# Attention with a pruned score mask: transposes and value products one unit later, the output copy in the slot of the last value products

## The chip, the core and the metric

One core of a Trainium2 chip runs the kernel. The metric is the device time of one execution in microseconds (us). The engines used are TensorE (PE in the profile; its weight loads are PEld), VectorE (DVE), ScalarE (ACT), GpSimd (POOL) and SyncE (SP), which issues all DMAs. Each engine works through its own program in order and is tied to the others by semaphores only.

## The reference, cut to what matters

```
x = in (8 batches, 512 tokens, 128 channels), f32;  xn = layernorm(x)
q, k, v = split(xn @ w_attn.T + b_attn);  16 heads of 8 channels
att = q @ k.T / sqrt(8), causal
S = relu(att of head 0), column 0 and diagonal set to 0
FF = cumulative sum of S down the rows, shifted by one row
att = att - FF                                    # the same FF for all heads
keep the 101 smallest FF of each row and the diagonal; the rest of att = -inf
y = softmax(att) @ v;  attn = y @ w_proj.T + b_proj
ffn = sum over the 2 chosen of 8 experts of gate * (relu(xn @ wi.T + bi + lora_e(xn)) @ wo.T + bo)
out = x + attn + ffn
```

## The kernel before, in words

The kernel takes the 8 batches one after the other. A batch's attention is cut into 44 **units** (`UNITS`, L58): a pair of a tile `a` of 128 queries (0 to 3) and so many heads that the scores fill one bank of PSUM: 4 heads for `a` = 0 (4 units), 2 for `a` = 1 (8 units), 1 for `a` = 2 and 1 for `a` = 3 (16 units each). `LAST` (L60) is the number of the last unit of each `a`: 3, 11, 27, 43. Four heads make a **group**; the group's last unit is marked in `ENDS_GROUP`.

Every engine's program is one loop over **slots** t (L514, L625, L902, L1144), one slot for each unit and some before and after. Unit u passes through these steps:

- PE, slot u, `score` (L851): the scores of unit u into one of three banks `ps_s`. It waits until VectorE has masked unit u-3 (L862).
- DVE, slot u (L1212): adds the mask, writes `ar` (a ring of 7) and the row maximum `mx`. POOL, slot u (L523), subtracts: the maximum minus the score.
- PE, slot u + LAG_T, `turn` (L868): transposes the unit into one of two banks `ps_t`; it waits for POOL (L871) and for the exponentials of unit u-2 (L875).
- ACT, slot u + LAG_T (L682): the exponentials, `pr` (a ring of 6).
- PE, slot u + LAG_P, `weigh` (L881): for the last unit of a group, the value products of four heads into the one bank `ps_o`. The first group of the next `a` waits until that bank was copied out (L887).
- ACT, slot LAST[a] + LAG_P + OUT_LAG (L694): copies `ps_o` to `out_t`, after the wait for all value products of that `a` (L696).
- PE, "ot{a}", slot LAST[a] + LAG_P + OT_LAG (L825): transposes `out_t`; DVE divides by the sums in the same slot (L1190). "yt{a}" (L831) comes two slots after it, "proj1" two more after yt3 (L84 to L86). "proj0" stands at slot 40.

In a slot PE does, in this order, score(t), turn(t - LAG_T), the jobs of the slot (`fill`), weigh(t - LAG_P). ACT does the jobs that it reads, the exponentials, the copy of `ps_o` if it is due, and then its part of the preparation of other batches (`act_prepares`). DVE does its jobs, the mask of unit t, and then preparation.

The jobs are everything that is no attention unit: the feed-forward part of the batch (z at slot 5, mask0 and mask1 at 7 and 8, the hidden layers h00 to h31 at slots 14 to 24, two products each from L807 and L811, down0 and down1 at 28 and 30), and the preparation of the next batches (s0 to s3 at 15 to 18, v at 16, f0 to f3 at 20 to 23, then on DVE and ACT a search for a threshold from slot 24 on, L1030 to L1061, and the choice of the largest values at slots 32 to 41; xt, q, k at 32, 34, 36; gate at 43, and its expert choice on DVE at slots 43 to 48). The search reads `nf`, which needs f3 on PE, DVE and POOL.

All jobs share two banks `ps_m`. `Plan` (L131 to L169) sorts the jobs by slot, within one slot by their place in the list (the feed-forward and output jobs stand ahead of the preparation), and gives the banks in turn; the two halves of a hidden layer keep one bank. A job waits until its bank's job before it has been read (L708).

SP issues the DMAs of the q and k stacks, x and the output (L417 to L425); the output's wait for proj0 and proj1.

Of the kernel before, what the change touches and what calls it, by code (L numbers as in the profile page):

```python
# [64 lines left out]
NS_RING, NT_RING, NM_RING = 3, 2, 2  # L65
NBANKS = NM_RING + NT_RING + NS_RING + 1
NA_RING, NP_RING = 7, 6
LAG_T, LAG_P = 3, 4
OUT_LAG, OT_LAG, YT_LAG = 1, 2, 4
TAIL = 13  # L70

QUAD = 4
# [1215 lines left out]
```

How the kernel before makes its waits and increments, by code:

```python
            def wait_full(eng, name, k):  # L345
                eng.wait_ge(m_full, full(name, k))
# [1 line left out]
            def wait_read(eng, name, k):  # L349
                who, n = plan.reads[name, k]
                eng.wait_ge(act_read if who == "act" else dve_read, n)
# [17 lines left out]
                @block.sync  # L370
# [1 line left out]
                    def fetch(m):  # L372
                        if m >= 1:
                            sp.wait_ge(x_in, 16 * m)
                        if m >= XN:
                            wait_read(sp, "down1", m - XN)
                        sp.dma_start(xs[:, m % XN, :, :],
                                     x_d[bass.ds(m, 1)].rearrange("o p a c -> p (o a) c")).then_inc(x_in, 16)
# [1 line left out]
                    def make_stacks(m):  # L381
                        if m >= 2:
                            sp.wait_ge(scored, NU * (m - 1))
                        else:
                            sp.wait_ge((zeroed, zeroed_1)[m], 2)
                        for t in range(2):
                            sp.wait_ge(split, 2 * m + t + 1)
                            stack, part = ((qs, Q_PART), (ks, K_PART))[t]
                            for j in range(len(part)):
                                sp.dma_start(stack[8 * j:8 * j + 8, into(m), :, :],
                                             parts[:, t, part[j], :]).then_inc(stacked, 16)
# [19 lines left out]
                    make_stacks(1)  # L412
                    fetch(2)
                    sp.wait_ge(w_prep, 2)
                    for j in range(2):
```

## Time and profile before

| | |
|---|---|
| time, median of 3 runs | 747.84 us (745.73 to 748.78) |
| profiled execution | 753.04 us, span 751.2 us |
| PE busy | 601.0 us, 80% of the span |
| DVE busy | 538.1 us, 72% |
| POOL busy | 437.9 us, 58% |
| ACT busy | 380.8 us, 51% |
| mean granted TensorE clock | 0.931 of full speed |

The profiled execution is the source of all rows below; its own time is 5.2 us above the median of the runs. The first scores start at 61.0 us and the last at 736.4 us, so a batch takes some 85 us. No engine is busy all the time. A share of busy time over the whole span therefore doesn't tell which engine sets the time of a stretch, and the stretches have to be looked at one by one.

### The profile page before, as it was taken

Reading aid. Unit: us, or ns where it says so; the run is one execution under the profiler, and the core shown is the slowest. Engines: PE = TensorE matmul, PEld = TensorE weight load, DVE = VectorE, ACT = ScalarE, POOL = GpSimd, SP = SyncE. Lnnn points to the kernel's source line nnn. Section 1 sums busy time; section 2 is a strip of 40 time slices with the busy share of each in tenths; the row PEclk is TensorE's granted clock in tenths of the full one; section 3 lists DMA queues with packets and bytes.
Section 4 is the critical chain, followed back from the end, with each engine's and each line's share of the span. In section 5 each row is a group of like instructions: output and inputs, shape, how many; then the busy total and the mean of one; then the engine's idle time right before and its main releaser. Section 6 shows DMA issues by size and latency. Waiting matters only on the chain. (4 is left out here: it accounts for less than half of the span.)

```text
span 751.2 us, 16859 instructions
## 1 busy us (share of the span) xinstructions
PE 601.0 (80%) x5495; PEld 405.7 (54%) x5495; DVE 538.1 (72%) x2256; ACT 380.8 (51%) x813; POOL 437.9 (58%) x739
## 2 busy tenths in 40 slices
PE   4536798779887888779988888778887798779895
PEld 1314456556565656466565655556564564656474
DVE  7685648975599756995589856996479855985352
ACT  3444346445563555644564545645464555535542
POOL 6408455575736865376655856378554857348451
PEclk9866899899998899989998999999998999989998
DMA  4151620052001500034000520025000430000000
GB/s 88 19 58 20 67 23 16 1 68 33 1 16 29 64 8 1 16 49 52 1 15 12 63 28 2 15 37 63 3 1 2 59 41 1 2 12 5 2 1 15
DMA packets 27286, 18.98 MB, mean 25 GB/s; under 512 B 5417, under 2 KB 27072, under 8 KB 27200
## 3 DMA queue, kind: packets, MB, share of 16 engines
q1 hardware_dynamic: 27200, 17.91, 18.2%
q8 instruction: 45, 0.74, 0.4%
q14 instruction: 41, 0.34, 0.2%
HBM read 3.22 MB, written 2.10 MB: 7 GB/s over the span
## 5 line engine op out<-in xcount | busy, mean ns | idle before, releaser
L523 POOL TENSOR_SCALAR ar<-ar,mx 128x512 f32<-128x512 f32 (+3 forms) x512 | 282.1, 561 | 245.8 <-DVE mx L1221 244.5
L1221 DVE CUSTOM_DVE_ANT_0 ar<-ps_s,mask 128x512 f32<-128x512 f32 (+3 forms) x512 | 231.1, 484 | 52.1 <-PE ps_s L864 49.5
L877 PE MATMUL ps_t<-ident,ar 128*128 128x128 f32 x1280 | 212.2, 286 | 33.6 <-POOL ar L523 18.4
L690 ACT ACTIVATE pr<-ps_t 128x512 f32<-128x512 f32 (+1 forms) x352 | 190.9, 554 | 86.1 <-PE ps_t L877 85.1
L877 PEld LDWEIGHTS ps_t<-ident,ar 128*128 128x128 f32 x1280 | 160.4, 147 | 79.7 <-POOL ar L523 58.3
L864 PE MATMUL ps_s<-ks,qs 96*128 96x512 bf16 (+3 forms) x512 | 134.2, 315 | 31.0 <-DVE mx L1221 22.8
L896 PE MATMUL ps_o<-pr,va 128*32 128x128 f32 x2560 | 104.7, 295 | 27.3 <-ACT out_t L699 14.6
L896 PEld LDWEIGHTS ps_o<-pr,va 128*32 128x32 f32 x2560 | 67.3, 116 | 62.6 <-ACT pr L690 41.5
L675 ACT ACTIVATE h<-ps_m,bi_col 128x512 f32<-128x512 f32 x64 | 44.0, 687 | 101.5 <-PE ps_m L811 101.5
L864 PEld LDWEIGHTS ps_s<-ks,qs 96*128 96x128 bf16 x512 | 43.4, 100 | 80.8 <-DVE mx L1221 36.2
L811 PE MATMUL ps_m<-zm,b_t 128*128 128x512 f32 x128 | 66.9, 604 | 5.2 <-ACT h L675 5.2
L618 ACT ACTIVATE junk<-nf,cut 128x384 bf16<-128x384 f32 x64 | 42.2, 662 | 25.0 <-DVE cut L1058 20.9
L1221 DVE DVE_READ_ACCUMULATOR2_ANT mx<- 128x1 f32 x512 | 41.9, 82 | 0.0
L1171 DVE TENSOR_SCALAR_CACHE_REDUCE nf<-ps_m 128x128 f32<-128x128 f32 (+3 forms) x28 | 13.7, 491 | 38.0 <-PE ps_m L788 38.0
L537 POOL TENSOR_TENSOR hsum<-h 128x512 f32<-128x512 f32 x32 | 40.5, 1266 | 0.4 <-DMA bias_rows<-hsum 0.4
L807 PE MATMUL ps_m<-xnt,wi_t 128*128 128x512 f32 x64 | 34.3, 618 | 1.9 <-DVE va L1157 1.9
L811 PEld LDWEIGHTS ps_m<-zm,b_t 128*128 128x128 f32 x128 | 22.0, 192 | 24.6 <-issue 15.9
L1021 DVE TENSOR_TENSOR_SCAN ft<-ones,s 128x511 f32<-128x511 f32 (+3 forms) x32 | 28.7, 897 | 5.0 <-POOL s L494 3.8
L823 PE MATMUL ps_m<-wo_t,hsum 128*128 128x128 f32 x256 | 31.2, 275 | 0.0
L1113 DVE MATCH_REPLACE8 work<-top,work 128x144 f32<-128x144 f32 (+1 forms) x64 | 31.0, 493 | 0.0
L823 PEld LDWEIGHTS ps_m<-wo_t,hsum 128*128 128x128 f32 x256 | 29.9, 192 | 0.2
L1105 DVE MAX8 top<-work 128x8 f32<-128x144 f32 (+1 forms) x64 | 29.4, 500 | 0.7
(215 smaller groups left out, 780.2 us busy)
## 6 DMA issues: line engine op xcount, KB each, us to landing
qs<-parts SPq DMA_DIRECT2D x48, 128.0 KB
ks<-parts SPq DMA_DIRECT2D x48, 128.0 KB
xs<-in_L_attn_x SPq DMA_DIRECT2D x8, 256.0 KB, 3.0
out<-res SPq DMA_DIRECT2D x8, 192.0 KB, 2.0
out<-res SPq DMA_DIRECT2D x8, 64.0 KB, 6.4
ar<-in_L_ffn_wi SPq DMA_DIRECT2D x1, 256.0 KB, 3.3
ar<-in_L_ffn_wo SPq DMA_DIRECT2D x1, 256.0 KB, 3.9
ar<-in_L_ffn_lora_B SPq DMA_DIRECT2D x4, 64.0 KB, 4.1
```

The lines of the kernel that those rows point to most:

```text
L523: nc.gpsimd.tensor_scalar(col, col, -1.0, mx[:, t % NA_RING, j:j + 1], ALU.mult, ALU.add)\
L537: nc.gpsimd.tensor_tensor(hsum[:, f, :], h[:, 2 * (f % 2), :], h[:, 2 * (f % 2) + 1, :], ALU.add).then_inc(h_sum, 1)
L618: nc.scalar.activation(junk[:, a - 2, 0:P * (a + 1)], nf[:, OFF[a]:OFF[a + 1]], ACT.Sign, bias=cut[:, a:a + 1], scale=-1.0, accum_out=abov ...
L675: nc.scalar.activation(h[:, 2 * (f % 2) + j, :], m[:, :], ACT.Relu, bias=bi_col[:, f:f + 1])\
L690: nc.scalar.activation(pr[:, u % NP_RING, 0:w], ps_t[u % NT_RING][:, 0:w], ACT.Exp, scale=-1.0)\
L807: nc.tensor.matmul(m[:, :], wi_t[:, P * f:P * f + P], xnt[:, n % 2, :], start=True, stop=False)
L811: last = nc.tensor.matmul(m[:, :], b_t[:, P * f:P * f + P], zm[:, j, :], start=False, stop=True, skip_group_check=(j == 1))
L823: last = nc.tensor.matmul(m[:, P * a:P * a + P], hsum[:, f, P * a:P * a + P], wo_t[:, f, :], start=False, stop=(a == hi - 1 and f == NF - 1))
L864: last = nc.tensor.matmul(ps_s[u % NS_RING][:, w * j:w * j + w], qs[:, k % 2, h0 + j, P * a:P * a + P], ks[:, k % 2, h0 + j, 0:w], start=T ...
L877: last = nc.tensor.transpose(ps_t[u % NT_RING][:, P * j:P * j + P], ar[:, u % NA_RING, P * j:P * j + P], ident[:, :])
L896: last = nc.tensor.matmul(ps_o[OW * j:OW * j + OW, P * group:P * group + P], va[:, k % 2, c, VW * hh:VW * hh + OW], pr[:, (NU * k + unit) ...
L1221: nc.vector.tensor_tensor_reduce(out=ar[:, t % NA_RING, w * j:w * j + w], in0=ps_s[t % NS_RING][:, w * j:w * j + w], in1=mask[:, k % 2, OF ...
```

## The change

```
-LAG_T, LAG_P = 3, 4
-OUT_LAG, OT_LAG, YT_LAG = 1, 2, 4
+LAG_T, LAG_P = 4, 5
+OUT_LAG, OT_LAG, YT_LAG = 0, 2, 4
```

Transposes and exponentials of unit u move from slot u+3 to slot u+4 on PE and ACT, value products from u+4 to u+5 on PE. The copy of `ps_o` stays in slot LAST[a] + 5 of ACT, which was 4 + 1 and is 5 + 0; the last value products that it reads are now in that same slot on PE. The jobs ot, yt and proj1 move one slot on, on PE and on the engine that reads them:

```
        ot0 ot1 ot2 ot3   yt0 yt1 yt2 yt3   proj1     (slot of their batch)
before    9  17  33  49    11  19  35  51    53
after    10  18  34  50    12  20  36  52    54
```

Slots 49 to 54 are slots 5 to 10 of the next batch. By the rule of `Plan` the banks of some jobs change with it: before, slot 17 held h10, ot1, s2, slot 18 h11, s3, slot 19 yt1, slot 20 h20, f0. After, slot 17 holds h10, s2, slot 18 h11, ot1, s3 with s3 in the bank of h11, and slot 20 h20, yt1, f0 with f0 in the bank of yt1. mask1 stands in the bank of mask0, where it stood in that of yt3. No instruction is added or removed.

## Rows read from the trace of the kernel before

**Rows 1.** Waits: engine, waiting line, releaser: us in total, times, longest.

```profile
PE ps_s L864 <- DVE mx L1221: 22.8, 25, 3.0
PE ps_o L896 <- ACT out_t L699: 14.6, 7, 2.5
```

**Rows 2.** Windows of the fourth batch and its border: busy us of each engine, granted clock.

```profile
294.40:338.50 44.10, 34.08 (x360) 25.09 (x353) 41.86 (x185) 24.70 (x54) 25.45 (x45) 0.91 0.19 28
338.50:379.80 41.30, 37.78 (x316) 24.42 (x315) 22.52 (x92) 20.84 (x44) 27.23 (x47) 0.97 0.21 24
337.80:340.50 2.70, 2.70 (x19) 2.25 (x20) 0.62 (x4) 0.36 (x1) 2.62 (x7) 0.50 0.56 57
```

**Rows 3.** Timeline of PE at two borders: start, us, instruction [idle before, releaser].

```profile
333.47 1.08 PE L896 MATMUL ps_o<-pr,va 128*32 128x128 f32 x32
334.49 0.39 PE L864 MATMUL ps_s<-ks,qs 96*128 96x256 bf16 x2
337.80 0.66 PE L896 MATMUL ps_o<-pr,va 128*32 128x128 f32 x8 [2.48 <-ACT out_t L699]
345.64 0.38 PE L864 MATMUL ps_s<-ks,qs 96*128 96x256 bf16 x2
...
597.63 0.43 PE L896 MATMUL ps_o<-pr,va 128*32 128x128 f32 x8 [2.49 <-ACT out_t L699]
604.00 0.38 PE L864 MATMUL ps_s<-ks,qs 96*128 96x256 bf16 x2
```

**Rows 4.** Timeline of ACT at the first of these borders.

```profile
335.42 0.23 ACT L590 ACTIVATE expd<-less 128x36 f32<-128x36 f32 x1 [1.24 <-DVE less L1001]
336.59 0.58 ACT L690 ACTIVATE pr<-ps_t 128x512 f32<-128x512 f32 x1
337.07 0.59 ACT L699 ACTIVATE out_t<-ps_o 128x512 f32<-128x512 f32 x1
```

**Rows 5.** Timeline of DVE at the same border.

```profile
336.14 0.08 DVE L1221 DVE_READ_ACCUMULATOR2_ANT mx<- 128x1 f32 x1
...
338.30 0.22 DVE L1012 TENSOR_TENSOR vsum<-vsum,den 128x4 f32<-128x4 f32 x1
340.79 0.26 DVE L1196 RECIPROCAL rec<-ps_m 128x16 f32<-128x16 f32 x1 [2.27 <-PE ps_m L829]
```

**Rows 6.** Timeline of PE, slots 15 to 21 of the fifth batch.

```profile
355.49 1.10 PE L811 MATMUL ps_m<-zm,b_t 128*128 128x512 f32 x2 [0.38 <-ACT h L675]
...
359.85 1.12 PE L807 MATMUL ps_m<-xnt,wi_t 128*128 128x512 f32 x2 [0.32 <-DVE va L1157]
...
362.94 0.28 PE L777 MATMUL ps_m<-qs,ks 96*128 96x256 bf16 x1 [0.68 <-DVE y L1198]
...
366.00 0.86 PE L896 MATMUL ps_o<-pr,va 128*32 128x128 f32 x24 [0.31 <-ACT pr L690]
...
370.05 1.10 PE L811 MATMUL ps_m<-zm,b_t 128*128 128x512 f32 x2 [0.27 <-ACT h L675]
```

**Rows 7.** Timeline of ACT in the same slots.

```profile
354.66 0.69 ACT L675 ACTIVATE h<-ps_m,bi_col 128x512 f32<-128x512 f32 x1 [2.56 <-PE ps_m L811]
...
365.82 0.29 ACT L549 ACTIVATE yt<-ps_m 128x128 f32<-128x128 f32 x1
```

**Rows 8.** The chain that ended last: start, us, work without its waits.

```profile
680.67 0.44 PE ps_m L829 x4
...
693.11 0.86 PE ps_m L807 x2
```

**Rows 9.** Timeline of four engines, slots 23 to 25: start of the search.

```profile
375.05 0.86 PE L896 MATMUL ps_o<-pr,va 128*32 128x128 f32 x24
376.99 0.46 POOL L500 TENSOR_TENSOR nf<-nf,causal 128x128 f32<-128x128 f32 x1
378.37 0.61 ACT L618 ACTIVATE junk<-nf,cut 128x384 bf16<-128x384 f32 x1
379.87 0.93 DVE L1055 TENSOR_TENSOR step_to<-row_len,above 128x4 f32<-128x4 f32 x1 [1.01 <-ACT junk L618]
```

## The prediction

> **What bounds the kernel now.** I read the page first, then the table of waits, then the windows of one batch, and then the timelines of PE, DVE and ACT where the windows show a change of engine. The page shows no engine at its full share, so the reader has to look for stretches. The windows give two for each batch [rows 2]. From 294.4 to 338.5 us DVE is busy 41.9 of 44.1 us, with next to no wait in its timeline: this half (search, choice of the largest values, expert choice, slots 25 to 48) is VectorE's. From 338.5 to 379.8 us PE is busy 37.8 of 41.3 us and DVE only 22.5: this half (slots 49 to 68, in the next batch's own count 5 to 24) is TensorE's. The pattern stands in seven borders between batches; the last batch prepares nothing and is PE's nearly throughout. A PE wait counts only in the second half, or where DVE stands because of it.
>
> The table of waits names the candidates [rows 1]. PE's wait for `mx`, 22.8 us, lies mostly in DVE's half. The wait of the value products for the output copy, 14.6 us in 7 pieces, lies exactly where the halves meet.
>
> **The border, step by step.** Slot 48 before: PE has done weigh(43) at 333.47, starts score(48) at 334.49, then turn(45), and stops, because weigh(44) needs `ps_o` free [rows 3]. ACT could have copied since 334.5, but in front of the copy it has the expert exponentials, which wait for DVE's choice until 335.42, the two wide copies, and an exponential at 336.59; the copy runs from 337.07 [rows 4]. PE resumes at 337.80 after 2.48 us. DVE runs out of work at 338.52 and waits 2.27 us for ot3 [rows 5].
>
> After: slot 48 on PE is score(48), turn(44), weigh(43). Weigh(43) is 1.0 us (its row has 1.08 with overlap). All this ends near 334.4. Then score(49) needs the mask of unit 46, and DVE reaches that only behind its expert choice: its fourth head ends at 336.22 [rows 5]. So PE still stands some 1.8 us, now for DVE, and goes on at 336.2. The copy, in the same ACT order as before, still ends near 337.7 (weigh(43) was long done). Between 336.2 and 337.7 PE has score(49), turn(45) and z: some 0.2 (a score's row overlaps what follows it), 0.44 for four transposes and 0.86 for two products of 512 columns [rows 8], 1.5 us in all, which covers the copy. PE thus restarts 337.80 - 336.2 = 1.6 us earlier. From there to score(53) the same kinds of work follow as before from weigh(44) on (turn(45) in place of turn(49)). New short waits come in: weigh(45) stands behind the copy, a mask relu and the read of z on ACT, some 0.25 us; mask1 now shares the bank of mask0, which DVE reads only after its mask of unit 50, some 0.4 us. Net 1.6 - 0.65 = 1.0 us a border.
>
> The clock comes on top. In the 2.7 us after the stall the granted clock was 0.50 [rows 2], the lower level, 1.2 GHz, after PE had stood 2.48 us. Weigh(44) to score(53) then took 345.64 - 337.80 = 7.84 us; at the sixth border after an equal stall without a fall it took 604.00 - 597.63 = 6.37 us [rows 3]. So a fall costs 1.4 us. Five of the seven borders show slow matmuls near by, two show none. The Trainium skill ("TensorE: Matmul & The Clock Gate", section "What's actually happening") says that the clock goes by how busy PE has been of late and that half speed is the resting state. The trace agrees at the fourth border but not at the sixth, so the rule alone doesn't fix this sum. The stall shrinks from 2.5 to 1.8 us, so I count 0.2 us a border, between 0 and 1.4.
>
> Term A: 7 x (1.0 + 0.2) = 8.4 us. Its lower bound is 0 (the copy or the exponentials of ACT end late whatever PE does, and the two borders whose stall is short give little); the upper is 7 x 2.5 = 17.5 us (no 0.4 us wait, hence 1.3, and most of the clock).
>
> **PE's half, the job banks.** The later value products now stand between jobs that wait for each other. Weigh of offset 9 moves behind h00 and covers the 0.38 us before h01; that of offset 11 moves behind v and covers the 0.32 us before h10; s2 no longer waits for ot1's division, 0.68; the weigh at slot 63 loses its 0.31 by moving behind f0; h21's 0.27 goes too [rows 6]. Removed: 1.96 us a batch, for the seven batches that prepare a next one. Added: s3 takes the bank of h11 and needs ACT's read. Such a read holds PE from 354.66 to 355.49 [rows 6, 7], 0.83 us and its start, less the 0.44 us of ot1's four transposes [rows 8]: 0.4 us. And f0 takes the bank of yt1, in the same slot behind h20: ACT must first read h20 (0.69) and then yt1 (0.29) [rows 7], while PE has only one transpose, 0.1, to do: 0.95 us with the releases. Net 1.96 - 1.35 = 0.6 us; I take 0.4. Term B: 7 x 0.4 = 2.8 us, between -2.8 (only 0.68 and 0.31 are really lost) and 8 (most of the new waits covered).
>
> **The start of the search.** h31's relu stands on ACT before the search's first counts, and DVE waits 1.01 us for these [rows 9]. Weigh(19), 24 products and 0.8 us on PE at 375.05, stood between f3 and h31 and moves behind h31. h31 then comes 0.8 us earlier, and ACT reaches the counts near 377.5 in place of 378.37. They also need `nf` from POOL, 376.99 + 0.46 = 377.45, so no more than 0.9 us can come. I take 0.5 us in seven searches. Term C: 3.5 us, between 0 and 5.6. Late next is DVE's own count and mask, which run beside ACT's.
>
> **What costs nothing.** The `ar` ring: DVE in slot t needs turn(t-7), which PE does in slot t-3, ahead of score(t) in its order. `pr` and `ps_t`: LAG_P - LAG_T stays 1, so exponentials and their release keep their distance. ot2 and yt2 lie in DVE's half, where PE has room; if that cover were gone it would be their 0.44 us. The copy now waits in ACT for the value products of its own slot: at the border it is late anyway, in slots 8, 16 and 32 nothing of ACT's is due before the next PE job is filled. proj1 goes out one slot later; behind its wait on SP stand only a fetch of x for three batches on and the store of proj0, both far from due. POOL's order is untouched, and it gets a unit more of time before PE asks for it. At the end of the kernel one unit's transposes more come after the last score, which is earlier by as much: 0.
>
> **Sum.** 8.4 + 2.8 + 3.5 = 14.7 us. The profiled execution of 753.04 us (span 751.2) would be 738.3 us. It stood 5.2 us above the median, 747.84 us, from which the same sum gives 733.1: forecast 733 us.
>
> **The rivals.**
>
> *The stall only changes its name.* PE stands for `mx` in place of `out_t`, ACT's chain from the expert choice ends when it ended, and A is near 0, while B and C give 4 us together: 744 us. For it: DVE's half ends where DVE's work ends. Against: DVE itself waits 2.27 us for ot3 there [rows 5], so time is free.
>
> *Everything comes in.* 7 x 2.5 for the borders, 5 of B and 5 of C, 27.5 us: 720 us. For it: five borders show the slow clock; against: 1.8 us of standing stays.
>
> *ACT stands at the copy, and the kernel is slower.* The value products that the copy waits for now stand in its own slot: 1.0 us for the 32 of a = 3 (333.47 to 334.49 [rows 3]), in proportion 0.25, 0.5 and 0.75 for a = 0 to 2, 2.5 us a batch and 20 us in 8 batches. If reads of h, z and the exponentials behind it are what PE next waits for, all of that is on the path: 747.8 + 20 - 14.6 = 753 us. It decides from the point where ACT has less idle time than that around the copy. The order of ACT bears it out as a mechanism: the exponential at 336.59 stood behind a wait for DVE [rows 4]. Against: ACT is busy 20.8 of 41.3 us in PE's half [rows 2]. The Trainium skill ("TensorE: Matmul & The Clock Gate", section on the array's architecture) calls ScalarE's queue strictly first in, first out, which speaks for this rival.
>
> **How the numbers follow.** The forecast's case (724 to 742 us) gets 0.60, the stall that changes its name 0.20, everything 0.12, the slower case 0.08. A measurement of this kernel tells about 0.5% from no change, 744.1 to 751.6 us. The renamed stall lies on that edge and I split it in halves: faster 0.60 + 0.12 + 0.10 = 0.82, same 0.10, slower 0.08. The range goes from 720 to 745 us and leaves out the slower case and the ends of the others.
>
> **What would show it.** Right: the wait of L896 for `out_t` falls from 14.6 us to below 3; L864's wait for `mx` grows by 7 to 12 us; DVE's wait before L1196 at the borders falls below 1 us; a new wait near 1 us before f0's transposes (L788) and 0.4 before L777 of 96x128; the wait of L1055 for the counts halves. Wrong: if ACT shows waits for PE before L699 of 1 us and PE's waits for h or `pr` grow with them, the slower case holds; if the borders still take as long from score(48) to score(53), the first rival does.

## The result and the profile after

| | before | changed |
|---|---|---|
| time, median of 20 runs | 750.63 us (742.78 to 754.67) | 740.23 us (735.32 to 748.1) |
| ratio | | 0.9867, interval 0.9841 to 0.9892 |
| profiled execution | 753.04 us, span 751.2 | 735.32 us, span 733.5 |
| mean granted clock | 0.931 | 0.936 |

The change makes the kernel 1.3% faster, about 10 us. The ratio is that of the fast runs alone, the medians are over all twenty. The two profiled executions lie 17.7 us apart, more than the medians: that of before stands 2.4 us above its median and that of after 4.9 us below, so what follows is told by places, and sizes over the whole kernel are taken from the ratios.

The table of waits of the changed kernel has engine, waiting line, releaser, us in total, times, longest.

```profile
PE ps_s L864 <- DVE mx L1221: 32.8, 37, 1.8
PE ps_o L896 <- ACT pr L690: 18.5, 15, 2.5
PE ps_m L834 <- DVE y L1198: 13.1, 9, 3.4
PE ps_t L877 <- POOL ar L523: 8.6, 14, 0.9
PE ps_m L777 <- DMA ks<-parts: 7.3, 4, 2.8
PE ps_m L788 <- ACT yt L549: 5.9, 7, 0.8
DVE step_to L1055 <- ACT junk L618: 3.2, 9, 0.6
ACT out_t L699 <- PE ps_o L896: 2.8, 5, 1.2
```

Against [rows 1], the wait of L896 for `out_t` is gone, and the wait for `mx` has grown by 10 us. Two rows are new: L788 is f0 behind yt1, and L777 is s0, which waits for the DMAs that fill the q and k stacks of the next batch. The kernel before had no wait of that kind behind its start. Two waits that were small before have grown: the value products wait 18.5 us for exponentials (11.7 before) and yt 13.1 us for DVE's division (2.9 before). The long pieces, 2.5 us before the group's value products at 313.28 us and 1.3 us before yt2 at 301.46 us, lie in DVE's half, where PE waits anyway.

The timeline of PE at the third of the seven borders (the one at 337.80 us before, which the prediction calls the fourth) shows what stands in place of the stall of [rows 3]:

```profile
323.26 1.08 PE L896 MATMUL ps_o<-pr,va 128*32 128x128 f32 x32
326.07 0.39 PE L864 MATMUL ps_s<-ks,qs 96*128 96x256 bf16 x2 [1.73 <-DVE mx L1221]
327.69 0.42 PE L896 MATMUL ps_o<-pr,va 128*32 128x128 f32 x8
332.40 0.39 PE L864 MATMUL ps_s<-ks,qs 96*128 96x256 bf16 x2
...
350.24 0.23 PE L777 MATMUL ps_m<-qs,ks 96*128 96x128 bf16 x1 [0.34 <-ACT h L675]
354.59 0.33 PE L788 MATMUL ps_m<-ident,ft 128*128 128x128 f32 x1 [0.84 <-ACT yt L549]
...
512.15 0.38 PE L777 MATMUL ps_m<-qs,ks 96*128 96x512 bf16 x1 [2.58 <-DMA ks<-parts]
```

Weigh(43) is done first, then PE stands 1.73 us for the mask of unit 46, and weigh(44) at 327.69 does not wait at all. The same border on ACT and DVE, which answer to [rows 4, 5] and, with the second row of DVE, to [rows 9]:

```profile
325.21 0.23 ACT L590 ACTIVATE expd<-less 128x36 f32<-128x36 f32 x1 [2.42 <-DVE less L1001]
326.39 0.58 ACT L690 ACTIVATE pr<-ps_t 128x512 f32<-128x512 f32 x1
326.86 0.59 ACT L699 ACTIVATE out_t<-ps_o 128x512 f32<-128x512 f32 x1
```

```profile
329.36 0.26 DVE L1196 RECIPROCAL rec<-ps_m 128x16 f32<-128x16 f32 x1 [0.22 <-PE ps_m L829]
...
365.18 0.41 DVE L1055 TENSOR_TENSOR step_to<-row_len,above 128x4 f32<-128x4 f32 x1 [0.28 <-ACT junk L618]
```

ACT's chain is as late as before relative to DVE's choice: the copy still ends 1.1 us after the exponential starts. What has changed is that PE has work to do in that time. DVE waits 0.22 us for ot3 where it waited 2.27.

The clock is read from windows of 3 us: first five borders of the kernel before, then three of the same five of the changed one (the other two show 1.00 as well). The last columns are granted clock, DMA share and GB/s.

```profile
163.00:166.00 3.00, 2.10 (x16) 1.69 (x17) 1.52 (x10) 1.26 (x3) 2.92 (x9) 0.58 0.57 60
252.00:255.00 3.00, 3.00 (x14) 1.50 (x15) 1.23 (x6) 0.08 (x1) 2.78 (x6) 0.54 0.57 60
337.00:340.00 3.00, 2.20 (x16) 1.78 (x17) 1.42 (x10) 1.16 (x3) 2.92 (x9) 0.59 0.57 56
419.00:422.00 3.00, 2.65 (x36) 1.98 (x36) 2.71 (x12) 0.95 (x3) 2.75 (x7) 0.58 0.57 56
511.00:514.00 3.00, 3.00 (x19) 2.33 (x20) 1.07 (x6) 0.34 (x1) 2.85 (x6) 0.61 0.56 59
```

```profile
159.30:162.30 3.00, 2.99 (x26) 2.01 (x26) 2.86 (x19) 3.00 (x7) 3.00 (x9) 1.00 0.58 73
326.10:329.10 3.00, 3.00 (x26) 2.00 (x26) 2.86 (x20) 3.00 (x7) 3.00 (x9) 1.00 0.57 65
408.40:411.40 3.00, 3.00 (x26) 1.98 (x26) 2.86 (x20) 3.00 (x7) 3.00 (x9) 1.00 0.57 60
```

At the first, second, third and fifth border the clock stood near its lower level, 1.2 GHz, after a stall of 2.1 to 2.5 us. At the fourth the order is the other way round: the low stretch (0.52 from 420 to 423 us) lies ahead of the stall, which lasts 1.27 us, and PE goes on at full speed.

```profile
424.61 0.43 PE L896 MATMUL ps_o<-pr,va 128*32 128x128 f32 x8 [1.27 <-ACT out_t L699]
```

After the stall of 1.7 us in the changed kernel the clock stands at the full 2.4 GHz.

The period of a batch can be read off the start of `va`'s copy on DVE, one row for each batch:

```profile
262.18 0.88 DVE L1157 TENSOR_TENSOR va<-ps_m,bias_b 128x128 f32<-128x128 f32 x4 [4.09 <-PE ps_m L759]
344.48 0.88 DVE L1157 TENSOR_TENSOR va<-ps_m,bias_b 128x128 f32<-128x128 f32 x4 [2.67 <-PE ps_m L759]
...
513.95 0.88 DVE L1157 TENSOR_TENSOR va<-ps_m,bias_b 128x128 f32<-128x128 f32 x4 [5.07 <-PE ps_m L759]
600.83 0.88 DVE L1157 TENSOR_TENSOR va<-ps_m,bias_b 128x128 f32<-128x128 f32 x4 [6.12 <-PE ps_m L759]
```

One batch without a wait for the stacks takes 344.48 - 262.18 = 82.3 us; the one that ends at the last row takes 86.9 us. Before, five of the six such periods were between 86.6 and 87.3 us, and the sixth, whose border had no low clock, 85.0 us. The changed kernel thus has a faster batch, and something that keeps it from it in most batches.

### The profile page after: what moved, and what is told of

Its sections match the earlier page's. It is cut to its first block, busy times and chain, and to the rows that moved or that the text cites. A ratio compares the mean times of both kernels' runs of the same rounds, so it can differ in the third digit from the quotient of the medians.

```text
span 733.5 us, 16859 instructions
## 1 busy us (share of the span) xinstructions
PE 586.4 (80%) x5495; PEld 396.7 (54%) x5495; DVE 545.7 (74%) x2256; ACT 383.3 (52%) x813; POOL 437.3 (60%) x739
## 4 chain that ended last, share of the span: by engine, by line
PE 36%; DVE 18%; DMA 14%; issue 11%; ACT 9%; POOL 7%; SPq 5%; ACTq 0%; DVEq 0%; POOLq 0%
DMA ks<-parts 14%; PE ps_t L877 7%; PE ps_m L811 7%; PE ps_o L896 6%; SPq L391 5%; PE ps_s L864 4%; DVE ar L1221 4%; POOL ar L523 3%; PE ps_m L807 3%; ACT pr L690 2%; ACT junk L618 2%; ACT h L675 2%; DVE work L1096 2%; DVE work L1072 2%; ACT xn L586 1%
## 5 line engine op out<-in xcount | busy, mean ns | idle before, releaser
L877 PE MATMUL ps_t<-ident,ar 128*128 128x128 f32 x1280 | 205.3, 279 | 17.3 <-POOL ar L523 8.6
L877 PEld LDWEIGHTS ps_t<-ident,ar 128*128 128x128 f32 x1280 | 158.3, 144 | 52.2 <-POOL ar L523 25.2
L864 PE MATMUL ps_s<-ks,qs 96*128 96x512 bf16 (+3 forms) x512 | 133.1, 313 | 44.0 <-DVE mx L1221 32.8
L896 PE MATMUL ps_o<-pr,va 128*32 128x128 f32 x2560 | 102.8, 291 | 18.6 <-ACT pr L690 18.5
L896 PEld LDWEIGHTS ps_o<-pr,va 128*32 128x32 f32 x2560 | 66.1, 114 | 62.8 <-ACT pr L690 37.2
L864 PEld LDWEIGHTS ps_s<-ks,qs 96*128 96x128 bf16 x512 | 41.6, 100 | 89.6 <-DVE mx L1221 51.6
L811 PE MATMUL ps_m<-zm,b_t 128*128 128x512 f32 x128 | 66.5, 601 | 2.4 <-ACT h L675 2.4
L1021 DVE TENSOR_TENSOR_SCAN ft<-ones,s 128x511 f32<-128x511 f32 (+3 forms) x32 | 34.3, 1073 | 7.4 <-POOL s L494 6.5
L811 PEld LDWEIGHTS ps_m<-zm,b_t 128*128 128x128 f32 x128 | 21.7, 190 | 20.6 <-issue 15.5
```

Source lines behind the costliest of these rows:

```text
L811: last = nc.tensor.matmul(m[:, :], b_t[:, P * f:P * f + P], zm[:, j, :], start=False, stop=True, skip_group_check=(j == 1))
L864: last = nc.tensor.matmul(ps_s[u % NS_RING][:, w * j:w * j + w], qs[:, k % 2, h0 + j, P * a:P * a + P], ks[:, k % 2, h0 + j, 0:w], start=T ...
L877: last = nc.tensor.transpose(ps_t[u % NT_RING][:, P * j:P * j + P], ar[:, u % NA_RING, P * j:P * j + P], ident[:, :])
L896: last = nc.tensor.matmul(ps_o[OW * j:OW * j + OW, P * group:P * group + P], va[:, k % 2, c, VW * hh:VW * hh + OW], pr[:, (NU * k + unit) ...
```

## The experiments

All were timed in five rounds, and each ratio is to the kernel before on the same chip (748.3 us for the lags alone, the copy alone and the halved kernels with old and new lags, 748.7 us for the others).

**The lags alone.**

```
-OUT_LAG, OT_LAG, YT_LAG = 0, 2, 4
+OUT_LAG, OT_LAG, YT_LAG = 1, 2, 4        # LAG_T, LAG_P = 4, 5 kept
```

> The changed kernel with OUT_LAG back at 1: transposes four units behind the scores and value products five, the output copied one slot after the last value products. Theory one (the gain sits at the border, by the place of the copy in ACT's order): ACT then does the mask relu, the read of z and the exponentials of unit 45 before the copy, so the stall before weigh(44) comes back at the border, some 1.8 us in each of seven: about 752 us where the kernel before takes 750.6 and the changed one 740.2, less what the job banks and the search give, 746 to 750 us. Theory two (the deeper pipeline itself carries the gain, since TensorE waits less for GpSimd and for the search): 740 us, the wait for out_t small.

Measured: 744.46 us, ratio 0.9931 (0.9895 to 0.9967). The waits of PE:

```profile
PE ps_s L864 <- DVE mx L1221: 31.7, 35, 1.7
PE ps_o L896 <- ACT out_t L699: 12.3, 7, 1.8
```

The stall is back, 12.3 / 7 = 1.76 us a border where 1.8 was expected, behind the wait for `mx` that the deeper pipeline brings. The depth alone is worth some 5 us of 748; theory one holds, and the time is a little below its range. The clock did not fall at these borders, though PE worked for only 2.03 of 5 us around the third of them:

```profile
328.00:333.00 5.00, 2.03 (x16) 1.04 (x16) 4.15 (x29) 3.83 (x8) 4.59 (x13) 1.00 0.57 65
```

**The place of the copy alone.**

```
-LAG_T, LAG_P = 4, 5
+LAG_T, LAG_P = 3, 4                      # OUT_LAG = 0 kept
```

> The kernel before with OUT_LAG = 0 alone: lags 3 and 4, the copy in ACT's slot LAST + 4, together with the last value products. Theory one (the border): ACT now copies in slot 47, ahead of the expert exponentials that wait for VectorE, the 2.5 us stall before weigh(44) goes and PE waits some 1 us for the mask of unit 46 in its place: 739 to 743 us, near the changed kernel, and the waits of the job banks stay as before (0.68 before L777 and no wait before L788), the wait of L1055 stays 1.0 us. Theory two (the depth): 750 us. The slower rival of the prediction (ACT stands at the copy): above 752 us, with waits of L699 for PE near 1 us each.

Measured: 737.33 us, ratio 0.9825 (0.9784 to 0.9866).

```profile
PE ps_t L877 <- POOL ar L523: 24.9, 58, 1.6
PE ps_s L864 <- DVE mx L1221: 24.7, 31, 3.0
PE ps_o L896 <- ACT pr L690: 7.2, 15, 0.7
PE ps_m L811 <- ACT h L675: 5.2, 16, 0.4
PE ps_m L777 <- DMA ks<-parts: 1.9, 3, 0.9
```

```profile
DVE step_to L1055 <- ACT junk L618: 8.2, 9, 1.0
```

No wait of the value products for `out_t` is left, and the waits of the banks in PE's half and of the search stay as before, as theory one has it. At the border PE waits 0.5 us for the mask at three of six borders, less than the 1 us expected. Here too the stacks have become a wait, 1.9 us in three pieces. One number of three does what the whole change does; the intervals of the two overlap, so which is faster stays open. ACT stood at the copy for 6.9 us in 9 pieces, 1.3 at most, and that cost nothing that shows: the slower rival fell here, where the copy and its products stand closest.

The two halves give 13 and 5 us by their ratios, and the full change 10. They don't add up. The wait for the stacks, 7.3 us in the changed kernel and 1.9 us with the copy alone, is the suspect, and the next three kernels, which all leave out the same part of these transfers, test it.

**Half of the stack copies, on the changed kernel, on the one before and on the copy alone.**

```
-for j in range(len(part)):
+for j in range(0, len(part), 2):
-stacked, 192 * n                         # and the same factor in the other waits
+stacked, 96 * n
```

These kernels leave out every second stack copy (j = 1, 3, 5), and with it part of the products of q and k. The rows that are not filled are those of three of the six places, not all rows of the second and further parts as the first text below has it. The matmuls keep their number and size.

> The changed kernel with three of the six copies of q and of k into the stacks left out (rows of the second and further bf16 parts stay zero), so half the bytes of these DMAs. The trace of the changed kernel shows PE waiting for these transfers before s0 (L777) 7.3 us in four pieces and 2.3 us once more in a piece put down to issue, where the kernel before shows none. Theory: the stacks have become a bound of PE's half and take back 8 to 10 us. At the start of the kernel the first stacks are waited for too, so both half kernels win some 10 us there. This theory: 740 - 10 - 8 = 722 us, 16 to 20 us below the old kernel with the same halving. Rival (the transfers only fill time that another wait would take): 730 us, 10 us below it.

> The kernel before with the same three of six stack copies left out. In its trace no wait for the stacks stands before s0. Theory (stacks bound only the changed kernel): only the start is shorter, 750 - 10 = 740 us, and a batch's period stays 86.7 us. Rival (the stacks cost time in the kernel before as well, by their load on memory or on the order of SP): below 735 us and a shorter period.

> Lags 3 and 4 with OUT_LAG = 0, and three of the six stack copies of q and k left out, to be compared with the changed kernel under the same halving (725.7 us) and with the kernel before under it (747.2 us). Theory (place of the copy and depth add up, and the stacks hid this in the full kernels): between them, 733 to 736 us, some 9 us slower than with lags 4 and 5. Rival (the depth brings nothing by itself): 725 us.

| copies halved in all three | time | ratio |
|---|---|---|
| lags 3 and 4, OUT_LAG 1 (before) | 747.15 us | 0.9969 (0.9931 to 1.0007) |
| lags 3 and 4, OUT_LAG 0 | 733.22 us | 0.9801 (0.9764 to 0.9839) |
| lags 4 and 5, OUT_LAG 0 (changed) | 725.65 us | 0.9655 (0.9615 to 0.9694) |

With half the transfers the changed kernel loses its waits for the stacks and takes 0.9655 / 0.9969 = 0.9685 of the time of the old one, some 23 us, where with all of them it is 10 us. The place of the copy gives 0.9801 / 0.9969 = 0.983, the depth on top of it 0.9655 / 0.9801 = 0.985. With all copies the depth on top of the copy gives nothing that can be told from zero (0.9867 against 0.9825); with half it gives some 11 us, as the theory has it. That the depth and the copy are independent is not shown, for the depth without the copy was not run with half the transfers. With all of them it gave 0.9931, less than the 0.985, and its trace says why: the stall for `out_t` stays behind the new wait for `mx`. The depth brings its share only once the copy has moved.

Neither the kernel before nor the copy alone gains much from the halving: 0.9969, within its interval of no change, and 0.9801 against 0.9825. In the profile of the halved old kernel three of six periods are 85.4 us and not the 86.7 that were expected; at the borders of these batches the low clock lies ahead of a stall of 1.27 us, as at 424.61 above, and the gap told under **Open** is missing. In the halved new kernel three of six periods are that of the one undisturbed batch above, the others 83.0, 83.2 and 84.4 us. Its rows of `va` for two of the three are

```profile
177.11 0.88 DVE L1157 TENSOR_TENSOR va<-ps_m,bias_b 128x128 f32<-128x128 f32 x4 [2.67 <-PE ps_m L759]
259.36 0.88 DVE L1157 TENSOR_TENSOR va<-ps_m,bias_b 128x128 f32<-128x128 f32 x4 [2.67 <-PE ps_m L759]
341.60 0.88 DVE L1157 TENSOR_TENSOR va<-ps_m,bias_b 128x128 f32<-128x128 f32 x4 [2.67 <-PE ps_m L759]
```

They are 82.25 us apart. The expected 10 us at the kernel's start did not come: both missed their absolute times by it (725.7 for 722, 747.2 for 740). The waits of the old kernel with half the copies say why:

```profile
PE ps_s L864 <- DVE mx L1221: 20.3, 23, 3.0
PE ps_m L755 <- ACT parts L549: 7.1, 1, 7.1
```

The one wait of 8.3 us for the first stacks is gone and PE waits 7.1 us, once, for ACT's `parts` instead.

**The new bank waits taken out.**

```
-[(f"ot{a}", LAST[a] + LAG_P + OT_LAG, "dve") for a in range(NA)]
+[(f"ot{a}", LAST[a] + LAG_P + OT_LAG + (a == 1), "dve") for a in range(NA)]
-[(f"yt{a}", LAST[a] + LAG_P + YT_LAG, "act") for a in range(NA)]
+[(f"yt{a}", 26 if a == 1 else LAST[a] + LAG_P + YT_LAG, "act") for a in range(NA)]
```

> The changed kernel with yt1 at slot 26 and ot1 at slot 19, so that s3 no longer shares the bank of h11 nor f0 that of yt1 in one slot. Theory (the new bank waits of the change, 0.84 us before f0 and 0.34 us before s3, lie on the path in seven batches): 740 - 7 x 1.2 = 732 us, PE's wait of L788 for ACT below 1 us in total. Rival (the waits lie where DVE or the stacks set the time anyway, so they only move): 738 to 741 us.

Measured: 732.14 us, ratio 0.978 (0.9732 to 0.9829), the expected value. Against the changed kernel, by the two ratios, the gain is 0.9%, 6.6 us where 8.3 were worked out. L788 no longer waits for yt1. The waits for the stacks grew in this profile and ate at most a part of the gain:

```profile
PE ps_m L777 <- DMA ks<-parts: 10.2, 5, 3.2
PE ps_s L864 <- issue: 2.4, 1, 2.4
```

**The first reader of the stacks a slot later.**

```
-"s0": 15, "s1": 16, "s2": 17, "s3": 18, "v": 16, "scan0": 16, ... "scan3": 19,
+"s0": 16, "s1": 17, "s2": 18, "s3": 19, "v": 15, "scan0": 17, ... "scan3": 20,
```

> The changed kernel with s0 to s3 at slots 16 to 19 in place of 15 to 18, their scans one slot later, and v at slot 15 in place of 16: the first reader of the next batch's stacks stands a slot later. Theory (the landing of the stacks bounds slots 5 to 15 in the changed kernel, by up to 2.9 us a batch): a slot is some 2 us there, so most of the 9.6 us of waits for stacks goes and 732 to 735 us come out. Rival (the wait moves along, since what follows s0 to f3 on DVE becomes late by the same): 740 us.

Measured: 732.52 us, ratio 0.9776 (0.9733 to 0.9818).

```profile
PE ps_m L777 <- DMA ks<-parts: 3.8, 3, 1.6
PE ps_s L864 <- issue: 2.3, 1, 2.3
```

The wait fell from 7.3 to 3.8 us in these profiles and the time by 0.9%, 6.9 us, against the changed kernel. The edit also puts v ahead of s0, and how much of the gain that is was not separated. The gap of 2.3 us before L864, which the expectations counted with the stacks, is still there and lies before s0, so it is not the wait for their landing.

**Both.**

> Both edits together on the changed kernel: s0 to s3 one slot later with v ahead of them, ot1 at slot 19 and yt1 at slot 26. If both terms are independent: 740 - 8 - 7 = 725 us, the fastest so far with all work done. If a shorter border-to-border period brings the wait for the stacks back: 728 to 732 us.

Measured: 727.42 us (722.17 to 734.88), ratio 0.9702 (0.9654 to 0.9751): 3.0% below the kernel before with all of its work done, and about 1.7% below the changed one. It lies between the two expectations; the wait for the stacks is 3.1 us in its profile. It is the fastest full version that was run.

## Why the prediction was right, and where its sizes were off

**Direction, range and mechanism** held: faster was given 0.82, and 740.2 us lies within 720 to 745. The sum promised 14.7 us and 10 came, so the number was 7 us too fast, of which 2.8 us is the reference (747.84 us in three runs, 750.63 in twenty). That the sum came so near is in part luck: term A was too small by half, and the stacks, which took back about as much as it was short and some more, were not in it. The time is right, the account behind it has two errors of opposite sign.

**The border (term A).** Each step is in the trace. PE stands for `mx` 1.73 us where 1.8 was worked out, at six of the seven borders; the wait of L896 for `out_t` is 0, below the 3 that was named; the wait for `mx` grew by 10 us, within 7 to 12; DVE's wait for ot3 is 0.22 us, below 1. The two short waits that I charged, 0.65 us, don't show: from PE's restart to score(53) it takes 332.40 - 326.07 = 6.33 us, not 7.0. And the clock was mis-sized: I counted 0.2 us a border of a possible 1.4. Before, this stretch took 7.75 to 8.00 us at the four borders with the low clock behind the stall and 6.36 to 6.37 at the others; with the new lags it shows no low clock in any of the six profiles that were taken of them. That is some 1.4 us at four borders, 5.6 us, against the 1.4 us in the sum. At 7 borders x 1.6 us and 4 x 1.4 us the term is near 17 us rather than 8.4, at its upper bound. The short stall of the fourth border did not give less, as I had it: the value products before it were late by the low clock, PE went on 0.16 us before DVE's last operation of that half (424.61 against 424.77) where it was 0.50 at the third border, and in the changed kernel it is 2.0 at both. The seventh was not worked out. This is the step that failed in size, one half by the short waits and one half by the clock.

Why the clock stays up is not shown. It isn't the length of the stall by itself: with the lags alone PE stood 1.73 and then 1.76 us and the clock stayed at 1.00, while with the copy alone, where PE stood for 0.72 us at most between 148 and 156 us, it was 0.50 from 156 to 158 us, just before the first border.

**The banks (term B).** f0 waits 0.84 us (0.95 worked out), s3 0.34 us (0.4), each in nearly every batch. On the other side the wait of L777 for ot1's division is gone, and that of L811 for h fell from 5.2 us to 2.4 us. From score(53) to the first L1055 of the search it takes 379.87 - 345.64 = 34.23 us before and 365.18 - 332.40 = 32.78 in the undisturbed batch: 1.45 us less, for this term and the next together. With the 0.73 us of the search taken off, the banks give 0.7 us a batch and 5 us in all, where 2.8 were in the sum and 8 was the upper bound (the lower one, from its own two terms, should have been -2.5 and not -2.8). Taking the two new waits out gave 6.6 of 8.3 us, so they lie on the path for the most part.

**The search (term C).** DVE waits 0.28 us in place of 1.01, in seven batches, 5.1 us where I had 3.5 and an upper bound of 5.6. Not all of it is kept. The next small operations of DVE took longer:

```profile
381.05 0.16 DVE L1058 TENSOR_TENSOR cut<-step_to,goal 128x4 f32<-128x4 f32 x1
365.83 1.00 DVE L1058 TENSOR_TENSOR cut<-step_to,goal 128x4 f32<-128x4 f32 x1
```

Before (first row), L1055 and L1058 took 0.93 and 0.16 us, after (second row) 0.41 and 1.00, so 0.3 us of each 0.73 is lost again. Some 3 us are left, close to the forecast. Why they are longer was not looked into. DVE's half from there to the border, 44.9 us in an undisturbed batch before, is 45.2 us after, and in three of the seven batches 45.9 to 46.4, where DVE waits about 1 us more for a job of PE.

**What was missing: the stacks.** By its own terms as they came out, some 17, 5 and 3 us, the sum should have been near 25 us, and the kernels with half the stack copies show 23 us. The prediction put SP's twelve stack copies at nothing without naming them; its one remark on SP's order is that on proj1. They start when the scores of a batch are all done and are read at s0, slot 15 of the next batch. The old kernel reached s0 just after they had landed, so that its trace shows no wait:

```profile
353.00:354.00 1.00, 1.00 (x3) 0.38 (x2) 0.07 (x2) 0.00 (x0) 0.58 (x1) 1.00 0.10 10
354.00:355.00 1.00, 1.00 (x6) 0.49 (x4) 0.18 (x1) 0.34 (x1) 0.00 (x0) 1.00 0.00 0
356.42 0.38 PE L777 MATMUL ps_m<-qs,ks 96*128 96x512 bf16 x1
```

The DMA engines are idle from 354 us on and s0 starts at 356.42. At the six borders this distance is 0.8 to 3.8 us, and an undisturbed batch is some 4 us shorter between the border and s0 than before. What is taken out beyond the distance becomes a wait. That the copies take back the difference, about 13 us, is shown by the halving: the same change gives 0.9867 with all copies and 0.9685 with half. That they do it by landing late is shown for the part that stands as a wait, 7.3 us in four batches. The later reader gave 6.9 us back, which bears it out, with v moved as well. Whether their load costs something besides is not separated, but the profiles hint at it: the changed kernel took 735.32 us in its profiled execution and 724.96 with half the copies. Of these 10.4 us, 7.3 are the waits, 2.3 the gap told under **Open**, and some 0.8 us a stretch of low clock behind the longest wait (0.50 from 599.5 to 602 us). The profiled execution was a fast one, and how much more the others wait was not seen.

**The rivals.** The renamed stall: PE does wait for DVE, but 1.7 us and not 2.5, and DVE no longer waits for PE, so it fell. The slower case fell by ACT's own row: 2.8 us at the copy in the changed kernel, 6.9 us in the one with the copy alone, which was as fast. "Everything comes in", 720 us, came out near in its terms (25 of 27.5 us) and wrong in the time.

**Open.** A gap of 1.6 to 2.6 us before one score (422.66 us in the changed kernel), in which the profile names nothing that PE waits for, stands in the profiles of the five kernels with the new lags and all copies, and in none of the three with half of them. The two with the old lags and all copies have something like it at the same place of the same batch, before a transpose and put down to POOL:

```profile
437.69 0.66 PE L877 MATMUL ps_t<-ident,ar 128*128 128x128 f32 x4 [1.32 <-POOL ar L523]
```

With the copy alone it is 1.57 us. So the gap goes with the full transfers and not with the lags. What PE waits for there is open.

## What to carry to other kernels

Where two engines take turns as the bound, look at the border between their stretches: a short wait of the one for a third engine can be filled by moving work that is ready across it, and the place of one copy in an in-order engine's program can be worth more than a deeper pipeline. Before adding up what a shorter stretch gains, list every transfer that runs beside it and ask how long before its reader it lands: a transfer that shows no wait may have no slack. Two edits that together give less than one of them alone can point to such a hidden bound, and halving the suspected transfer in all kernels compared tests it. When a forecast comes out right, check its terms all the same: here two errors of opposite sign met.

## What the runs showed of the hardware

The granted clock over 3 us was 0.54 to 0.61 after PE stalls of 2.1 to 2.5 us at four borders of the kernel before, and 1.00 at the same four with the changed kernel's stall of 1.73 us. At the fourth border the low stretch, 0.52 from 420 to 423 us, came before the stall. A stall of 2.49 us at the sixth border left it at full speed in the kernel before, and so did 1.73 and 1.76 us in short succession with the lags alone, so the length of the stall alone doesn't decide. A low stretch behind the stall made the next 6.37 us of PE's work 1.4 to 1.6 us longer.

Twelve copies of 128 KB, issued by SP one after the other, took 27.5 us from the first issue to the landing that s0 waited for (232.87 to 260.38 us in the changed kernel), at a busy share of the DMA engines near 0.57.
